# Indirect DMAs of the expert phase: issued in ones to threes by step behind the last unit's gate product, the weighted sums a step later

## What is computed

```python
scores = sigmoid(xt @ gate_w.T)                    # 8192 tokens x 16 experts
_, idx = lax.top_k(scores + gate_b, 4)
w = take_along_axis(scores, idx); w = w / sum(w) * 2.5
for each expert e:
    h = silu(xt @ w1[e].T) * (xt @ w3[e].T)        # 128 hidden columns
    y += c[:, e] * (h @ w2[e].T)                   # c is w where e was chosen, else 0
y += the same body with the shared expert's weights
out = x + y
```

## Time and profile before

| | before |
|---|---|
| median of three runs | 2390.29 us |
| profiled execution, time | 2405.21 us |
| profiled execution, span | 2403.3 us |
| mean granted TensorE clock | 0.954 |
| attention phase | to about 1580 us |
| scatters of the expert phase | 1608.4 to 1787.5 us |
| gathers | 1890.9 to 2397.0 us |

### The profile page before, as it was taken

How to read it: one execution, slowest core, us unless ns; L and a number is a source line. 1 busy time by engine, 2 the same in 40 slices (tenths; PEclk the granted TensorE clock), 3 DMA queues, 4 the chain that set the end, 5 groups by cost and what they waited for, 6 DMA issues and landing times. The chain is left out here.

```text
span 2403.3 us, 58079 instructions
## 1 busy us (share of the span) xinstructions
PE 2132.9 (89%) x16576; PEld 2053.8 (85%) x16576; DVE 1878.6 (78%) x6129; ACT 1683.9 (70%) x4795; POOL 1405.8 (58%) x2107
## 2 busy tenths in 40 slices
PE   6999999999999999999999999977749777767775
PEld 5999999999999989999999899966749767767664
DVE  6999999999999999999999999973325355555567
ACT  5988888888989888888888898853326434334422
POOL 3555555555555558788877787666550244444455
PEclk8999999999999999999999999998869889989998
DMA  6777777777777668666665666666645457666676
GB/s 182 182 185 185 185 177 192 182 185 180 192 180 183 171 178 215 180 170 182 170 183 160 163 178 173 172 226 206 208 151 190 166 197 230 218 211 227 226 254 213
DMA packets 261295, 457.32 MB, mean 190 GB/s; under 512 B 36544, under 2 KB 148672, under 8 KB 260992
## 3 DMA queue, kind: packets, MB, share of 16 engines
q1 hardware_dynamic: 235376, 383.07, 57.6%
q0 software_dynamic: 25616, 70.55, 9.4%
HBM read 141.00 MB, written 144.70 MB: 119 GB/s over the span
## 5 line engine op out<-in xcount | busy, mean ns | idle before, releaser
L773 POOL TENSOR_SCALAR E<-E,rinv 128x256 f32<-128x256 f32 x1024 | 478.3, 478 | 461.6 <-DVE rinv L1084 457.3
L959 ACT ACTIVATE E<-E,negmax 128x256 f32<-128x256 f32 x1024 | 508.9, 502 | 4.9 <-DVE negmax L1109 4.8
L1521 POOL DMA_INDIRECT block<-expert_rows,slot x256 | 243.8, 953 | 365.7 <-DVE block L1775 129.9
L1109 DVE CUSTOM_DVE_ANT_0 E<-pS,m_in 128x256 f32<-128x256 f32 x1024 | 387.5, 416 | 35.9 <-PE pS L870 32.5
L1128 DVE TENSOR_TENSOR PT_lo<-pT,PT_hi 128x512 fp32r<-128x512 f32 x512 | 350.7, 685 | 27.9 <-ACT PT_hi L977 23.7
L977 ACT ACTIVATE PT_hi<-pT 128x512 fp32r<-128x512 f32 x512 | 304.9, 595 | 9.7 <-PE pT L880 0.4
L880 PE MATMUL pT<-ident,E 128*128 128x128 f32 x2048 | 306.6, 272 | 0.5 <-POOL E L773 0.5
L85 PE MATMUL epG<-w_hi,exT_hi 128*128 x608 | 198.2, 326 | 119.2 <-DVE exT_lo L1741 106.8
L893 PE MATMUL pV<-PT_hi,V 128*128 128x256 f32 x1024 | 287.6, 303 | 6.1 <-DVE PT_lo L1128 5.9
L1741 DVE TENSOR_TENSOR exT_lo<-epT,exT_hi 128x512 fp32r<-128x512 f32 x184 | 126.5, 688 | 207.8 <-ACT exT_hi L1655 155.9
L869 PE MATMUL pS<-qk_st 128*128 128x256 f32 x1024 | 268.8, 284 | 7.6 <-DMA qk_st<-qk_sp 7.4
(11 more groups left out here) (218 smaller groups left out, 7288.8 us busy)
## 6 DMA issues: line engine op xcount, KB each, us to landing
qk_st<-qk_sp SPq DMA_DIRECT2D x512, 192.0 KB
qk_st<-qk_sp SPq DMA_DIRECT2D x512, 128.0 KB
sorted_rows<-qk_st SPq DMA_DIRECT2D x152, 256.0 KB, 3.6
xg<-sorted_rows SPq DMA_DIRECT2D x76, 512.0 KB
expert_rows<-block SPq DMA_DIRECT2D x76, 512.0 KB
acc<-x_plus_attention SPq DMA_DIRECT2D x35, 256.0 KB
x_in<-in_x SPq DMA_DIRECT2D x32, 256.0 KB
c_in<-in_ctxT SPq DMA_DIRECT2D x32, 256.0 KB, 4.0
```

The source lines that it names most:

```text
L773: last = pool.tensor_scalar(e[:, t, :], e[:, t, :], rinv[:, r, t:t + 1], 1.0, ALU.mult, ALU.mult)
L959: last = act.activation(E[r][:, t, :], E[r][:, t, :], ACT.Exp, bias=negmax[:, r, t:t + 1], scale=-1.0, accum_out=rowsum[:, r, t:t + 1])
L1109: last = dve.tensor_tensor_reduce(out=E[r][:, t, :], in0=pS[g % 2][:, t, :], in1=m_in.tile(b)[:, t, :], scale=-1.0, scalar=BIG, op0=ALU.ad ...
L1521: pool.indirect_dma_start(out=cbuf[n % NCB][:, j, :], out_offset=None, in_=expert_rows[g], in_offset=bass.IndirectOffsetOnAxis(ap=shared.s ...
```

## The change

POOL's scatters and gathers are no longer issued a batch or a tile at a time. `scatter_at` and the new `gathers_at` hold single indirect DMAs, spread evenly over the steps: the 8 of a batch over 4.5 steps (so 1 or 2 a step, steps 6 to 68), the 4 of a tile over 1.82 steps (so 2 or 3 a step, steps 75 to 191). At each step that has any, POOL first waits in `keep_pace` until `s_GU` counts `worked(i - 1)` units, which is every unit up to i-2. The sums move from three to four steps after `gather_of` (COMBINE), and with them the stores of `acc` and the placement of the dense additions. The number of DMAs, their sizes, the buffers, the order of the units and the attention phase stay.

```diff
-    COMBINE = 3
+    COMBINE = 4
     TILE_STEPS, LANDED = 1.82, 6
     gather_of, at = [], 0.0
+    gathers_at = {}
     for n in range(B * NT):
         g = sum(n >= start * NT for start in GROUP_START[1:GROUPS])
         at = max(at + TILE_STEPS, sorted_end[g] - 1 + LANDED)
         gather_of.append(int(at))
+        for j in range(TOPK):
+            gathers_at.setdefault(int(at + j * TILE_STEPS / TOPK), []).append((n, j))
...
+    BATCH_STEPS = 4.5
     scatter_at = {}
     for b in range(scattered, B):
         g = sum(b >= start for start in GROUP_START[1:GROUPS])
-        at = len(PARKED) + 9 * (b - scattered) // 2
+        at = len(PARKED) + BATCH_STEPS * (b - scattered)
         if g == LATE_GROUP:
             at = max(at, PLACE_AT + 8 + 3 * (b - GROUP_START[g]))
-        scatter_at[at] = b
+        for n in range(NT * TOPK):
+            scatter_at.setdefault(int(at + n * BATCH_STEPS / (NT * TOPK)), []).append((b, n // TOPK, n % TOPK))
...
+            def keep_pace(i):
+
+                if worked(i - 1):
+                    pool.wait_ge(s_GU, worked(i - 1))
...
-                if i in scatter_at:
-                    if scattered < scatter_at[i] < LAST - 1:
-                        load_to_scatter(scatter_at[i] + 1)
-                    scatter(scatter_at[i])
-                for n in gather_at.get(i, ()):
-                    gather(n)
+                if i in scatter_at or i in gathers_at:
+                    keep_pace(i)
+                for b, t, j in scatter_at.get(i, ()):
+                    if t + j == 0 and scattered < b < LAST - 1:
+                        load_to_scatter(b + 1)
+                    scatter(b, t, j)
+                for n, j in gathers_at.get(i, ()):
+                    gather(n, j)
```

More of the change, by code:

```diff
@@ L1487, in load_to_scatter, with scatter @@
                 pool.dma_start(to_scatter[n % 2], rows_of(shared.xn_rows[b])).then_inc(s_toscat[n % 2], DMA)
-            def scatter(b):
+            def keep_pace(i):
+                if worked(i - 1):
+                    pool.wait_ge(s_GU, worked(i - 1))
+            def scatter(b, t, j):
                 g = sum(b >= start for start in GROUP_START[1:GROUPS])
                 n = b - scattered
[L1492 to L1498, removed]
-                rows = xn_last if b == LAST else to_scatter[n % 2]
[L1500 to L1523, removed]
+                if t + j == 0:
+                    if b == GROUP_START[g]:
+                        pool.wait_ge(router.s_slot, g + 1)
+                        pool.wait_ge(shared.s_zero[g], DMA * (2 * PAIRS_OF[g] * P // CLEAR_ROWS))
+                    if b == LAST:
+                        pool.wait_ge(s_norm, NORMED)
+                    else:
+                        pool.wait_ge(s_toscat[n % 2], DMA * (n // 2 + 1))
@@ new lines, in scatter, with gather @@
+                rows = xn_last if b == LAST else to_scatter[n % 2]
+                pool.indirect_dma_start(
+                    out=sorted_rows[g], out_offset=bass.IndirectOffsetOnAxis(ap=shared.slot[:, b * NT + t, j:j + 1], axis=0),
+                    in_=rows[:, t, :], in_offset=None).then_inc(shared.s_scat[g][b % 2], DMA)
+            def gather(n, j):
+                g = sum(n // NT >= start for start in GROUP_START[1:GROUPS])
+                if j == 0:
+                    if n == GROUP_START[g] * NT:
+                        for r in range(NYS):
+                            stored = [q for q in range(first_c[g + 1] // 2) if q % NYS == r]
+                            pool.wait_ge(s_yst[r], DMA * len(stored))
+                    if n == 0:
+                        pool.wait_ge(s_w13lo, N_EXP)
+                        pool.wait_ge(s_w2lo, N_EXP)
+                        for b in range(B - 2, B):
+                            shared.scattered_here(pool, b)
+                    if n >= NCB:
+                        pool.wait_ge(s_cadd, n - NCB + 1)
+                pool.indirect_dma_start(
+                    out=cbuf[n % NCB][:, j, :], out_offset=None, in_=expert_rows[g],
+                    in_offset=bass.IndirectOffsetOnAxis(ap=shared.slot[:, n, j:j + 1], axis=0)).then_inc(s_cg[n % NCB], DMA)
```

## The result

The changed kernel took 2258.18 us in the median of four runs (2256.9 to 2262.02) against 2389.48 for the kernel before: a ratio of 0.9448 with a 95% interval of 0.9422 to 0.9475. That is faster, by 131 us. The forecast was 2230, and 160 us less than before. The profiled execution of the changed kernel took 2257.12 us, 1.9 more than its span.

The account below looks back on a forecast made before the run. TensorE was taken to bound the kernel, delayed after 1600 us while POOL issues indirect DMAs. Profiled 2405.2 less 164.7 saved plus 4 at the end gave 2244.5, less the 14.9 offset 2230 us; range 2135 to 2330.

Parts of the forecast that it names:

- Unbroken runs of indirect DMAs delay TensorE's semaphores: Expert phase: TensorE's semaphores are seen late while POOL issues indirect DMAs unbroken; 272.4 us over TensorE's own time.
- The line's zero at 2.3 DMAs: Excess by run length: 1.26 us for each further DMA, zero near 2.3, so pairs cost 0 and triples 0.9 us.
- Gathers, 3.55 us a unit: Gather stretch: between bounds 3.0 and 3.87, leaning up, 3.55 us a unit; 110 units make 390.5 us.
- Scatters, 3.2 us a unit: Scatter stretch: middle of bounds 2.8 and 3.44, 3.2 us a unit with a batch's load in it; 63 units, 201.6 us.
- keep_pace hidden: POOL's wait for a product two units back: four units, 14 us, cover 3.75 us of issue and 1.8 of landing.
- The end, 25.2 us: After the last unit: 15 gathers, landing, sum and store take 25.2 us against 21.3 before, so plus 4.
- The offset of 14.9 us: Whole kernel: the profiled execution before was 14.9 us over the median, so 2244.5 became 2230.
- DMA engines as the bound: Gather and scatter stretches: DMA engines become the bound, 3.9 us a unit among gathers, 3.5 among scatters; 2287 us, chance 0.21.
- Nothing is left: Expert phase: nothing is left of the delays, 2.9 us a unit everywhere, 251 us saved; 2139 us, chance 0.11.
- It doesn't do what it says: POOL's pairs, with gaps of 0.6 us, join into one run, each DMA costing 0.75 us as now; 2394 us, chance 0.06.
- A fixed price per group: Expert phase: every group costs 2.15 us whatever its length, 372 us for 173 units instead of 272; 2494 us, chance 0.09.
- POOL held by DVE: POOL's indirect DMAs each wait for one DVE operation of 0.69 us, spacing 1.94 us; 2337 us, chance 0.03.

Follow-up runs that it names:

- the first set: Changed kernel without keep_pace, kernel before with keep_pace ahead of whole bursts, changed kernel with COMBINE 3, kernel before with extra gathers: 2152.25, 2156.47, 2156.11, 2195.03 us.

## Why the prediction was right, and where its sizes were off

**Unbroken runs of indirect DMAs delay TensorE's semaphores** (the root of the forecast): that the excess goes with runs of indirect DMAs is shown. Seven plain ones cost 5.7 us where the line said 5.9, eights 7.2 where it said 7.2, direct loads nothing. Each half of the change without the other keeps most of the delay. Two things qualify it. DMAs 1.44 us apart cost about 0.6 of what they cost 1.25 us apart, so it isn't length alone. And not all of the excess is delay: by the estimate above, 60 of 277 us were TensorE at its lower clock, which the prediction counted as delay too. What delays the semaphores inside the chip stays open, and so does why the first set doesn't show it. Every execution on record has a profile's span and clock beside its time, so no run tells whether the delay is there when nothing is recorded.

**The line's zero at 2.3 DMAs** failed at its short end. The lower bound put a pair at 0; among gathers 43 of 97 intervals between silus are 3.09 to 3.24 us, about 0.35 over. The forecast's middle value between bound and bound absorbed this, which was luck and not working. With the pair at 0.35 and the line for the rest, the runs counted above make 59 x 0.35 + 10 x 0.9 + 3 x 2.1 + 10 x 3.4 = 70 us of excess from 1850 to 2200, against 350 - 98 x 2.8 = 75.6 measured. Half of it are the ten fives, which were not in the forecast: a triple lasts longer than the unit beside it, so that the next pair follows with no gap. With the pairs and triples as planned a unit would have come to 2.8 + (4 x 0.35 + 0.9) / 5 = 3.26 us.

**Gathers, 3.55 us a unit:** 3.58 measured, 394.1 us for the 390.5 of the sum.

**Scatters, 3.2 us a unit:** 3.47 measured; this is the term that was mis-sized most, 211.9 us for 61 units where the sum had 201.6 for 63. "(a batch's load is in it)" was the step that failed: the load's duration was counted and its wait was not. With the waits ahead of a batch now in the middle of an evenly spread row, POOL stops once a batch, and in the catch-up that follows the DMAs join into longer runs. The listed runs from 1608 to 1816 give, by the line and with pairs at 0.35, 46 us; measured were 205 - 59 x 2.8 = 39.8 in the window from 1610 to 1815. At 3.2 it would have been 24. This is read from the timelines; no kernel without that wait was run.

**Spreading the scatters** into the quiet stretch: right, the quiet one shrank to 16.8 us. The forecast's 179 units in all were two too many: one is the table load in the earlier trace rows, and one comes of counting silus where the stretches between them are meant.

**keep_pace hidden:** right. POOL waits 95.2 us for products, DVE 5.9 us for gathers. **COMBINE 4, nothing:** not tested with the delay; without it the kernel with COMBINE 3 is within 0.3% of the one before.

**The end, 25.2 us:** 25.6, with 15 gathers behind the last unit as counted. By windows, POOL's indirect DMAs alone, kernel after:

```profile
2229.60:2255.20 25.60, 14.76 (x15) 0.59 0.51 164
```

**The offset of 14.9 us** between the profiled execution and the median was carried into the forecast. It was peculiar to that one execution of the kernel before: the profiled execution of the changed kernel lies 1 us below its median. The sum against profiled times was 2244.5 and 2257.12 was measured, 13 off; the subtraction of the offset added the rest of the 28.

**The rivals.** *DMA engines as the bound* (2287) is refuted by the 16-column gathers, 98 units at either traffic, and by 333 GB/s at a share of 0.96 in the set without the delay; 263 at 0.84 had been no ceiling. *Nothing is left* (2139) names a rate, 2.9 us a unit, that only the set without the delay shows. *It doesn't do what it says* (2394) happens when keep_pace is left out: 1.001. *A fixed price per group* (2494): a pair has a price after all, but 0.35 us and not 1.55. *POOL held by DVE* (2337), the rule of the Trainium skill, "SBUF — State Buffer", section "SBUF: two separate sides", isn't seen here. With DVE busy for 83% of the span the gathers take 947 ns in the median against 946 before; whether any operation of DVE here holds the shared port in the way that the page means, no run shows.

## What to carry to other kernels

If an engine waits for a sender without a name while another issues many DMAs of one kind, count the excess by length of run before blaming traffic; then break the runs up, and tie each piece to the progress of the engine that is delayed, since a piece with nothing to wait for joins its neighbour. After such a change look for the waits that are left in the issuing engine's order: any one that stops it for several us makes it issue the next pieces as one run. Look at the granted clock as well: a part of what a delay costs is slower work behind it. And run the kernel before again beside every set: the same kernel can have the problem in one set and not in another.

## What the runs showed of the hardware that was not expected

- The kernel before took 2150.21 us beside one set of runs and 2380.72 to 2395.61 beside the others, with nothing changed. The difference, 230 to 245 us, is most of the excess of the expert phase: the delay of TensorE's semaphores beside POOL's indirect DMAs was absent in the first. The split kernel without keep_pace was within 0.13% of before in it, and the changed kernel itself wasn't run there. What was different isn't known.
- A run of seven indirect DMAs cost no less with small rows: 5.7 us with rows of 1 KB, 6.6 us with rows of 64 bytes, each seen once. Seven direct loads issued by POOL cost nothing.
- TensorE's work after such a delay is slower: four transposes took 1.05 us at the lower clock and 0.60 at the higher.
- Gathers and TensorE at full rate can go together: 333 GB/s at a DMA share of 0.96 and a granted clock of 1.00 over 270 us, 2.97 us a unit.
- A load with a wait in POOL's order went with longer runs behind it, and so probably cost the change part of its gain. A third buffer for the rows to be scattered, so that the load needn't wait for the batch just issued, is the next step that the trace suggests; it wasn't tried.
